# Three routed feed-forward stages: how many projections TensorE computes ahead, and where their results are kept

## The reference

```python
x = x + jnp.tanh(g_xattn[0]) * _L0_xattn_ref(ctx_1024, _layernorm(x, axis=-1), ...)
x = x + jnp.tanh(g_ffn[0])   * _L0_ffn_ref(_layernorm(x, axis=-1), ...)
...  # layers 1, 2 and 3 likewise
```

```python
# layer 0: 16 experts (2 share a 128-column tile), top 4 of them, and a shared expert
combine = _route(x, gate_weight)                      # sigmoid, best groups, top 4, normalised
up = jnp.einsum('th,ehi->eti', x, expert_up)
down = jnp.einsum('eti,eih->eth', jax.nn.silu(up), expert_down)
moe_out = jnp.einsum('te,eth->th', combine, down)
return moe_out + jax.nn.silu(x @ shared_up) @ shared_down
# layer 2: 8 experts, softmax, top 2, one combining matrix after the weighted sum
expert_out = jax.nn.silu(jnp.einsum('nh,edh->ned', flat, expert_w) + expert_b)
out = (sum over the 2 chosen of weight * expert_out) @ combine_w.T
# layer 3: 32 experts (2 to a tile), sigmoid, top 6, and a shared expert
o = jax.nn.silu(xf @ g.T) * (xf @ u.T) @ dn.T        # per expert, times its weight, summed
```

## Time and profile before

| | before |
|---|---|
| median of 3 timed runs | 1203.96 us (1200.42 to 1205.02) |
| the profiled execution, its own time | 1199.11 us |
| its span, first to last instruction | 1197.4 us |
| mean granted TensorE clock | 0.984 of full |
| PE busy | 1110.3 us, 93% of the span |
| DVE, ACT, POOL busy | 742.4, 694.4, 473.6 us |

### The profile page before, as it was taken

The page is one execution under the profiler, slowest core; times in us unless marked ns, Lnnn a source line. Parts: engine busy times, 40 slices in busy tenths (PEclk is TensorE's granted clock), DMA queues, the critical chain, the costliest instruction groups (busy, mean ns, idle before and its releaser), DMA issues. The chain is left out here.

```text
span 1197.4 us, 24088 instructions
## 1 busy us (share of the span) xinstructions
PE 1110.3 (93%) x9673; PEld 809.9 (68%) x9673; DVE 742.4 (62%) x1386; ACT 694.4 (58%) x1225; POOL 473.6 (40%) x736
## 2 busy tenths in 40 slices
PE   3887999899999999999997989998979998999998
PEld 2553368788888888888885746664547664466667
DVE  6574556555655665566654269895559995645554
ACT  2576620565666566666665466777447777644440
POOL 4674001233333223443345353422473543644441
PEclk9999999899999999999999999999989999999999
DMA  9200000100000000000000000000000000032320
GB/s 341 80 1 1 1 1 2 71 2 1 2 2 1 2 1 1 2 1 2 1 1 1 1 1 2 2 2 1 2 1 2 2 2 1 7 96 99 95 82 19
DMA packets 13408, 27.93 MB, mean 23 GB/s; under 512 B 2641, under 2 KB 4977, under 8 KB 12530
## 3 DMA queue, kind: packets, MB, share of 16 engines
q1 hardware_dynamic: 13298, 26.39, 6.5%
HBM read 25.14 MB, written 1.25 MB: 22 GB/s over the span
## 5 line engine op out<-in xcount | busy, mean ns | idle before, releaser
L1213 POOL TENSOR_TENSOR work<-work 128x1024 f32<-128x1024 f32 x64 | 121.4, 1897 | 268.1 <-DVE work L1307 268.1
L1294 DVE TENSOR_REDUCE work<-psum 128x8 f32<-128x1024 f32 x64 | 78.0, 1219 | 86.2 <-PE psum L1093 86.2
L1235 ACT ACTIVATE work<-work 128x1024 f32<-128x1024 f32 x64 | 67.4, 1053 | 96.2 <-DVE work L1298 96.2
L1305 DVE TENSOR_REDUCE work<-work 128x8 f32<-128x1024 f32 x64 | 77.4, 1209 | 71.9 <-ACT work L1235 71.9
L1672 PEld LDWEIGHTS psum<-w_down,work 128*128 128x128 f32 x768 | 99.4, 191 | 28.7 <-issue 27.2
L1672 PE MATMUL psum<-w_down,work 128*128 128x128 f32 x768 | 100.6, 275 | 0.7 <-DVE x L1789 0.7
L958 ACT ACTIVATE work<-psum 128x512 f32<-128x512 f32 x128 | 72.9, 596 | 46.1 <-PE psum L827 45.3
L998 DVE TENSOR_REDUCE work<-psum 128x8 f32<-128x1024 f32 x64 | 75.2, 1216 | 22.1 <-PE psum L813 22.1
L827 PEld LDWEIGHTS psum<-ident,work 128*128 128x128 f32 x512 | 56.7, 142 | 43.7 <-ACT work L955 21.5
L1298 DVE TENSOR_TENSOR work<-psum,work 128x1024 f32<-128x1024 f32 x64 | 78.4, 1225 | 6.7 <-DVE work L1294 0.5
L827 PE MATMUL psum<-ident,work 128*128 128x128 f32 x512 | 75.3, 280 | 7.2 <-ACT work L958 5.9
(11 more groups left out here) (336 smaller groups left out, 2552.3 us busy)
## 6 DMA issues: line engine op xcount, KB each, us to landing
work<-chosen SPq DMA_DIRECT2D x80, 128.0 KB, 3.0
x<-in_x SPq DMA_DIRECT2D x2, 512.0 KB, 4.5
ctx_tok<-in_ctx SPq DMA_DIRECT2D x2, 512.0 KB, 6.6
xnt<-in_xt SPq DMA_DIRECT2D x1, 1024.0 KB, 9.0
ctxt<-in_ctxt SPq DMA_DIRECT2D x1, 1024.0 KB, 11.0
mask<-in_mask SPq DMA_DIRECT2D x1, 1024.0 KB, 10.0
w_down<-in_down SPq DMA_DIRECT2D x1, 1024.0 KB, 8.4
ctx_tok<-in_g SPq DMA_DIRECT2D x1, 1024.0 KB, 4.9
```

The source lines that it names most:

```text
L1213: pool.tensor_tensor(prob[:, u % 2, h, :], prob[:, u % 2, h, :], rinv[:, u % 2, h].unsqueeze(2).broadcast_to([P, 8, P]), ALU.mult)\
L1235: act.activation(p, p, ACT.Exp).then_inc(S["exp"], 1)
L1294: dve.tensor_reduce(nmax[:, u % 2, h], s, AX.X, ALU.max, negate=True).then_inc(S["max"], 1)
L1305: dve.tensor_reduce(rsum[:, u % 2, h], prob[:, u % 2, h, :], AX.X, ALU.add).then_inc(S["sum"], 1)
```

## The change

It passes ahead = 32 for 20 in f0, 28 for 12 in f2 and 30 for 16 in f3. The ring grows with it, from 23, 15 and 19 slots to 35, 31 and 33. The additional slots lie in tiles that hold nothing at that time: in f0 in `negb`, `mask2` and the space of `w["down3"]`, in f2 and f3 in layer 1's attention weights, layer 0's expert weights and (f3) `ew2`. The ring's line now cuts a spare tile by its own width. As `mask2` and `down3` serve f0 as ring slots, their two loads (1 MB each) move from `load_weights` to the loads of ab1, in front of and behind those of g3 and u3.

```diff
+FIRST = ("wq0", "wkv0", "wo0")
+DEFERRED = ("g3", "u3", "down3")
@@ weights_of_layer
-        if (...) == s and n not in ("wq0", "wkv0", "wo0", "g3", "u3"):
+        if (...) == s and n not in FIRST + DEFERRED:
             yield k.w[n][:, :], k.dram[n]
-    if s == 2:
-        yield k.mask2[:, :], k.dram["mask2"]
@@ wide_attention, sync
-        for dst, src in loads:
-            sp.dma_start(dst[:, :], src).then_inc(k.late[3], 16)
+        for dst, src, layer in loads:
+            sp.dma_start(dst[:, :], src).then_inc(k.late[layer], 16)
@@ feed_forward
-    ring = [one[:, n * GT:(n + 1) * GT] for one in spare for n in range(NG)][:R]
+    ring = [one[:, at:at + GT] for one in spare for at in range(0, one.shape[1], GT)][:R]
@@ build
+        deferred = [(k.mask2, dram["mask2"], 2), *((w[n], dram[n], 3) for n in DEFERRED)]
+        wide1 = [w[n] for n in ("wq1", "wk1", "wv1", "wo1")]
 # f0
-  ahead=20, lags=(1, 3, 4), requantise=Requantise, spare=(k.ctx_tok, *k.big),
+  ahead=32, lags=(1, 3, 4), requantise=Requantise,
+  spare=(k.ctx_tok, *k.big, k.negb, k.mask2[:, :].bitcast(F32), w["down3"]),
 # f2
-  ahead=12, lags=(4, 7, 8), on_act=True, one_down=True, spare=(k.big[0], k.big[2], k.negb),
+  ahead=28, lags=(4, 7, 8), on_act=True, one_down=True,
+  spare=(k.big[0], k.big[2], k.negb, *wide1, w["up0"], w["down0"]),
 # f3
-  ahead=16, lags=(0, 0, 0), spare=(k.big[0], k.big[2], k.negb, k.ctxt),
+  ahead=30, lags=(0, 0, 0),
+  spare=(k.big[0], k.big[2], k.negb, k.ctxt, *wide1, w["up0"], w["down0"], w["ew2"]),
```

More of the change, by code:

```diff
@@ L222 @@
 SMALL = {"afc": (16, 128), "bfct": (16, 512), "aproj": (16, 512), "bprojt": (16, 128)}
+FIRST = ("wq0", "wkv0", "wo0")
+DEFERRED = ("g3", "u3", "down3")
 def weights_of_layer(k, s):
     for n in [*WEIGHTS, *SMALL]:
-        if (int(n[-1]) if n[-1] in "0123" else 1) == s and n not in ("wq0", "wkv0", "wo0", "g3", "u3"):
+        if (int(n[-1]) if n[-1] in "0123" else 1) == s and n not in FIRST + DEFERRED:
             yield k.w[n][:, :], k.dram[n]
-    if s == 2:
-        yield k.mask2[:, :], k.dram["mask2"]
     if s == 3:
@@ L1062, in sync @@
         sp.wait_ge(k.late[2], k.late_count[2])
-        for dst, src in loads:
-            sp.dma_start(dst[:, :], src).then_inc(k.late[3], 16)
-            k.late_count[3] += 16
+        for dst, src, layer in loads:
+            sp.dma_start(dst[:, :], src).then_inc(k.late[layer], 16)
+            k.late_count[layer] += 16
         yield
@@ L2024, in build @@
         up3 += [(w["sg3"][:, :], None, w["su3"][:, :], None, w["sd3"][:, :])]
-        g3u3 = [(w["g3"], dram["g3"]), (w["u3"], dram["u3"])]
+        deferred = [(k.mask2, dram["mask2"], 2), *((w[n], dram[n], 3) for n in DEFERRED)]
+        wide1 = [w[n] for n in ("wq1", "wk1", "wv1", "wo1")]
         def f0(prev):
-            return feed_forward(k, prev, "f0", 1, up0, ACT.Silu, ahead=20, lags=(1, 3, 4), requantise=Requantise,
-                                spare=(k.ctx_tok, *k.big),
+            return feed_forward(k, prev, "f0", 1, up0, ACT.Silu, ahead=32, lags=(1, 3, 4), requantise=Requantise,
+                                spare=(k.ctx_tok, *k.big, k.negb, k.mask2[:, :].bitcast(F32), w["down3"]),
                                 routing=dict(E=16, groups=4, top_groups=2, top=4, kind="sigmoid", gate_w=w["gate0"],
@@ L2033, in ab1 @@
         def ab1(prev):
-            return wide_attention(k, prev, "ab1", k.big[0], g3u3)
+            return wide_attention(k, prev, "ab1", k.big[0], deferred)
         def f1(prev):
@@ L2045, in f2 @@
         def f2(prev):
-            return feed_forward(k, prev, "f2", 5, up2, ACT.Silu, ahead=12, lags=(4, 7, 8), on_act=True, one_down=True,
-                                spare=(k.big[0], k.big[2], k.negb),
+            return feed_forward(k, prev, "f2", 5, up2, ACT.Silu, ahead=28, lags=(4, 7, 8), on_act=True, one_down=True,
+                                spare=(k.big[0], k.big[2], k.negb, *wide1, w["up0"], w["down0"]),
                                 routing=dict(E=8, groups=None, top_groups=None, top=2, kind="softmax",
@@ L2056, in f3 @@
         def f3(prev):
-            return feed_forward(k, prev, "f3", 7, up3, ACT.Silu, ahead=16, lags=(0, 0, 0),
-                                spare=(k.big[0], k.big[2], k.negb, k.ctxt),
+            return feed_forward(k, prev, "f3", 7, up3, ACT.Silu, ahead=30, lags=(0, 0, 0),
+                                spare=(k.big[0], k.big[2], k.negb, k.ctxt, *wide1, w["up0"], w["down0"], w["ew2"]),
                                 routing=dict(E=32, groups=8, top_groups=4, top=6, kind="sigmoid", gate_w=w["gate3"],
```

## The result

| | before | after |
|---|---|---|
| median of 6 timed runs each, same chip | 1200.68 us (1197.95 to 1205.02) | 1210.54 us (1208.35 to 1216.48) |
| ratio after to before | | 1.0087, 95% interval 1.0067 to 1.0107 |
| span of the profiled execution | 1197.4 us | 1208.8 us |
| mean granted clock | 0.984 | 0.974 |

The account below looks back on a forecast made before the run. PE, busy 93%, was taken as the bound, with other engines limiting parts without projections. Terms -1.0 + 5.5 + 2.5 + 2.7 = +9.7 us on 1203.96 gave 1213.7, rounded 1214, range 1204 to 1221.

Parts of the forecast that it names:

- What bounds it: Whole kernel: PE busy 93%, so moves pay only where PE waits; added projections can fill only f3's 0.97 us.
- f3 ahead of the loop, -1.0: In f3 before `turn_back(0)`: 14 more projections remove PE's wait of 0.97 us; -1.0 us, other bound 0.
- f2, +5.5: f2's main loop: a second turn wait +3.0, group 0's end +0.9, half-rate clock +1.6; ends 2 and 8 us.
- f0, +2.5: f0 steps 11 to 22: DVE becomes the bound, and group ends wait; +2.5 us, ends 0 and 5.
- Moving a projection is free for PE as such: Price of a step: a projection is 0.86 us wherever it stands; what it stood before loses that cover.
- f3's row of downs, +2.7: f3 steps 38 to 51: 14 downs in a row wait for tiles SP brings by DMA; +2.7 us, ends 0.5 and 5.0.
- Seven more tiles at 1.25: f3's row: after tile 42, tiles through 49 come at SP's issue pace of 1.25 us each, giving 13.9 for tile 49.
- The weigh at 0.94 or 1.50: f3's row: at 0.94 us DVE's weigh adds nothing, at 1.50 it makes 7.0 of the 2.7; the shorter was taken.
- The loads, 0: From 211 us on, beside ab1: moving the loads of `mask2` and `down3` costs 0 us.
- Hardly anything: Rival, chance 0.22: waits only change place, DVE and POOL keep up at the other group ends; +1.5 to +5 us.
- Faster: Rival, chance 0.07: f2's idle time breaks into short gaps, both turn waits vanish; -6.7 us, 1197.
- Much slower: Rival, chance 0.18: f3's weighs stay at 1.50, f2 pays in full, f0 goes at DVE's pace; +18 us, 1222.

Follow-up runs that it names:

- The run with the late turn: Against the kernel with loads moved and f2's ahead at 28, f2's turns stand 12 steps behind instead of 8; 1202.06 us, f2 62.69 us.
- two kernels with the same wait: Both with f2's 12 ahead and early turn: f3's tiles 38 on by select (1203.75 us), and f0's Requantise pieces at every second step (1202.31 us).
- the kernel with the loads alone: Against the kernel before, only the loads of mask2 and down3 moved beside ab1, all ahead numbers unchanged; 1199.79 us, ratio 0.9991.
- f2's part alone: Against the kernel before, the two loads moved and only f2's ahead raised, from 12 to 28; 1208.59 us, ratio 1.0061.
- f3's part alone: Against the kernel before, the two loads moved and only f3's ahead raised, from 16 to 30; 1204.67 us, ratio 1.0025.

## Why the prediction was right, point by point

- **What bounds it.** Right: the wait of 0.97 us ahead of `turn_back(0)` was all that there was to fill, and the stages lose in the parts without projections.
- **f3 ahead of the loop, -1.0.** Right, 0.97 gone.
- **f2, +5.5.** Right in mechanism: waits at both turns (3.03 and 3.38 for the one of 3.01), 1.29 at group 0's end, two half-rate stretches for one. Measured +6.6. The turn waits grew by 3.4 where I had 3.0, so the clock and the pace of the pairs, with the group ends, cost 3.2 where I had 2.5. The run with the late turn shows what hangs on the turns: 5.1 us, with the clock of its execution. What the prediction could not say is how likely the half-rate stretch is: two kernels with the same wait have none.
- **f0, +2.5.** Measured +2.05. The new waits are 0.68 + 0.17 us as the profile marks them, and by differences of starts, which leave the modelled ends out, 179.99 - 178.25 - 0.89 = 0.85 and 184.02 - 181.80 - 2 x 0.89 = 0.44: together 1.3, not 2.5. Another 0.66 is a term that I did not have: the 12 projections in the row took (152.91 - 123.44) - (141.02 - 122.53) = 10.98 us, 0.915 each, and not the 0.86 at which they stood in the loop. "Moving a projection is free for PE as such" fails by that; in f2 the long row runs at 0.87. The row of before shown above had this pace already and could have been read. The sign that DVE runs without pause there held, from 172.8 to 185.3 us. The size came out right in part by luck: one term was half of what I took, another I had left out.
- **f3's row of downs, +2.7.** This is the term that was mis-sized: it measured +4.9. The path was right up to tile 42: weigh by landing, landing by freed slot, first wait after about seven tiles. "Seven more tiles at 1.25" failed. I took SP's issues for the pace of the landings, with 3.0 us from issue to landing throughout. The issues do go at 1.26 a tile, but the time to landing grows from 3.2 to 4.9 us, and from the first weigh that waits for a landing to the eighth it is 1182.19 - 1171.56 = 10.63 us, 1.52 a tile, where I had 8.75. That is 1.9 of the 2.2 us that I was short. The high end of my range, 5.0, had that number, by bytes at 160 GB/s; the number was right and its reason was not, since half the bytes take as long. The low end took a shortest landing of 1.6 us, which was none of the spreads'.
- **The weigh at 0.94 or 1.50.** It fell to 0.69 as soon as POOL had no products left. The rule cited from "SBUF — State Buffer" of the Trainium skill held here: the trace agrees, 0.69 in the row against 1.50 at 1163.74.
- **The loads, 0.** Right: 0.9991 (0.9975 to 1.0007).
- **The sum.** +9.7 was forecast, the spans differ by 11.4 and the medians by 9.9. The terms make +12.7 for the three stages (2.05 + 6.6 + 4.0); outside them the spans differ by +0.9, -2.3 and +0.1, together -1.3, of which the -2.3 is the clock (last section). That the forecast of 1213.7 is 3 us above the 1210.5 measured comes from its base: 1203.96 was the median of three runs, and the kernel before has 1200.7 in the six beside the change.
- **The rivals.** "Hardly anything" needed DVE and POOL to keep up at group 0's end, and f2 shows them late there. "Faster" needed no wait at the turns. "Much slower" needed weighs of 1.50.

## What to carry to other kernels

Work that is moved ahead fills only the wait it is put in front of; read that wait first (here 0, 0 and 0.97 us), and then count what the moved work had covered. Where transfers fill a ring and a run of steps is faster than they are, take the supply's pace from landings and not from issues, and count a further slot as one full period of it. Where a turn or a normalisation stands a fixed number of steps behind its cause, that number has to grow when the steps get shorter: four more steps gave 0.4% even without the change. Whether that was the wait or the clock behind it has to be read from more than one execution.

## What the runs showed of the hardware that I had not expected

**The clock differs from execution to execution in places where the code is the same.** The windows of f2 under "the same in the kernel before" show it. At ab1's start before has a stretch at half rate that after lacks. The 2.3 us between f0 and f2 are that: the kernel with the loads alone, whose ab1 is after's, has it, and 609.99 us there as before has 610.02. Windows in before and in after:

```profile
221.00:228.00 7.00, 5.64 (x24) 5.34 (x25) 2.15 (x3) 2.67 (x5) 1.90 (x1) 0.52 0.01 2
```

```profile
212.00:224.00 12.00, 9.57 (x96) 8.83 (x94) 7.05 (x17) 5.22 (x7) 2.04 (x6) 1.00 0.71 287
```

In six of the fourteen profiled executions a0, ahead of f0, has 27 us in a row at half rate, as here in the kernel with f2's part alone:

```profile
98.00:125.00 27.00, 23.37 (x101) 12.89 (x102) 8.49 (x31) 12.40 (x33) 9.10 (x31) 0.50 0.00 1
```

f0 starts some 5 us later in these (126.9 to 129.6 against 120.9 to 123.4). One of them is the kernel before but for f2's turn, so no edit is behind it. In a comparison of single executions such a stretch outweighs most terms of this case; stage by stage it can be told apart.

**A transfer's pace need not be its bytes.** 128 KB or 64 KB to 64 partitions, two a tile: 1.52 us a tile in the changed kernel and 1.57 with f3's part alone, 1.56 with half the bytes, where the windows of the first and the last have a DMA share of 0.80 and 0.45. And one transfer in place of two can be three times slower, if its outer dimension is small.
